# Attention and FFN in one kernel: other order of loads and clearings, gate and up weights by column halves, statistics behind the last block, twelve dummy transposes

## The reference

```python
xn = layernorm(x)                          # x: (16, 256, 256) float32, last axis 256
q, k, v = split(xn @ w_qkv)                # 16 heads of 16
attn = softmax(where(causal, q @ k.T / 4, -1e10)) @ v
a = attn @ w_out
gate, up = qdot(xn, w_gating[0]), qdot(xn, w_gating[1])   # operands cast to float8 e4m3; 256 -> 1024
f = qdot(gelu(gate) * up, w_linear)                       # 1024 -> 256
out = x + a + f
```

## Time and profile before

| | us |
|---|---|
| median of 3 runs | 421.89 (421.83 to 424.61) |
| the profiled execution, its own time | 421.3 |
| its span, first to last instruction | 419.6 |
| FFN stage up to the first matmul of `project_qk` | 103.28 |
| PE busy / DVE / ACT / POOL in the span | 371.5 / 296.7 / 223.9 / 106.9 |

### The profile page before, as it was taken

The page is one execution under the profiler, slowest core; times in us unless marked ns, Lnnn a source line. Parts: engine busy times, 40 slices in busy tenths (PEclk is TensorE's granted clock), DMA queues, the critical chain, the costliest instruction groups (busy, mean ns, idle before and its releaser), DMA issues.

```text
span 419.6 us, 9896 instructions
## 1 busy us (share of the span) xinstructions
PE 371.5 (89%) x3646; PEld 275.6 (66%) x3646; DVE 296.7 (71%) x1325; ACT 223.9 (53%) x320; POOL 106.9 (25%) x138
## 2 busy tenths in 40 slices
PE   5796589999899779999999999999999999889774
PEld 5253345556475567778788788787787787667443
DVE  5876197776545887788788888887887887787112
ACT  2773266665555145655655655556556556455540
POOL 2131033332021113322232232223323222333320
PEclk9897899999999989999999999999999999998885
DMA  7999332340717343461551642633624613300000
GB/s 244 295 352 208 110 102 100 121 181 2 247 55 252 125 160 111 139 212 47 201 180 51 229 149 80 230 113 115 228 83 148 228 49 133 104 28 2 28 25 26
DMA packets 45943, 57.58 MB, mean 137 GB/s; under 512 B 2568, under 2 KB 38984, under 8 KB 45896
## 3 DMA queue, kind: packets, MB, share of 16 engines
q1 hardware_dynamic: 45896, 56.96, 40.9%
HBM read 16.78 MB, written 12.58 MB: 70 GB/s over the span
## 4 chain that ended last, share of the span: by engine, by line
PE 68%; DVE 9%; DMA 6%; SPq 5%; issue 5%; ACT 5%; POOL 1%; POOLq 0%; ACTq 0%; DVEq 0%
PE ps L721 12%; PE ps L646 11%; PE ps L700 9%; PE ps L682 7%; PE ps L752 7%; PE ps L653 6%; PE ps L634 5%; PE ps L737 4%; DMA xt_store<-xt_part 3%; DVE act L377 3%; DMA xres<-in_L_attn_x_dram 3%; PE ps L744 2%; PE ps L614 2%; DVE masked L415 2%; SPq L192 2%
## 5 line engine op out<-in xcount | busy, mean ns | idle before, releaser
L415 DVE CUSTOM_DVE_ANT_0 masked<-ps,causal 128x256 bf16<-128x256 f32 (+1 forms) x512 | 149.1, 350 | 35.3 <-PE ps L682 35.3
L542 ACT ACTIVATE arena<-ps 128x1024 f32<-128x1024 f32 x96 | 98.7, 1028 | 76.9 <-PE ps L700 76.5
L307 POOL TENSOR_SCALAR_AFFINE_SELECT arena<-arena 128x512 f32<-128x512 f32 (+1 forms) x96 | 75.8, 789 | 191.5 <-ACT arena L542 191.5
L377 DVE TENSOR_TENSOR act<-ps,gate 128x512 fp8e4<-128x512 f32 x64 | 43.8, 684 | 18.8 <-ACT gate L495 18.0
L700 PE MATMUL ps<-stack 64*128 64x256 f32 (+1 forms) x512 | 51.7, 301 | 5.1 <-ACT arena L542 3.8
L721 PE MATMUL ps<-arena,v_aug 128*32 128x256 f32 (+1 forms) x1024 | 54.4, 343 | 1.2 <-POOL arena L307 1.2
L646 PE MATMUL ps<-xs,wq_part 128*128 128x256 f32 x384 | 53.4, 290 | 1.5 <-issue 0.7
L682 PE MATMUL ps<-stack 63*128 63x256 f32 (+1 forms) x512 | 49.1, 291 | 5.4 <-DVE row_max L415 5.4
L607 PE MATMUL ps<-x,wg 128*128 128x512 fp8e4 x128 | 40.2, 397 | 11.1 <-ACT x L483 4.9
L646 PEld LDWEIGHTS ps<-xs,wq_part 128*128 128x128 f32 x384 | 47.9, 191 | 2.7 <-ACT ffn L515 1.2
L495 ACT ACTIVATE gate<-ps 128x512 bf16<-128x512 f32 x64 | 38.1, 599 | 18.5 <-PE ps L607 14.0
(11 more groups left out here) (52 smaller groups left out, 377.1 us busy)
## 6 DMA issues: line engine op xcount, KB each, us to landing
stack<-qk_part SPq DMA_DIRECT2D x96, 256.0 KB, 2.8
xt_store<-xt_part SPq DMA_DIRECT2D x16, 512.0 KB, 4.2
xs<-xt_store SPq DMA_DIRECT2D x16, 512.0 KB, 4.1
out_dram<-w_raw SPq DMA_DIRECT2D x16, 256.0 KB, 2.8
xres<-in_L_attn_x_dram SPq DMA_DIRECT2D x1, 2560.0 KB, 13.6
arena<-in_L_ffn_w_gating_dram SPq DMA_DIRECT2D x2, 1024.0 KB, 8.6
stack<-zeros SPq DMA_DIRECT2D x4, 512.0 KB, 12.6
xres<-in_L_attn_x_dram SPq DMA_DIRECT2D x2, 512.0 KB, 12.2
```

The source lines that it names most:

```text
L307: nc.gpsimd.affine_select(diag, diag, pattern=[[0, 1024 // width], [1, P]], compare_op=ALU.is_ge, fill=0.0, base=0, channel_multiplier=-1) ...
L377: nc.vector.tensor_tensor(act8[:, j, :], up_ps[j % 2][:], gate[:, j % 2, :], ALU.mult, saturate=False).then_inc(act_done, 1)
L415: last = nc.vector.tensor_tensor_reduce(masked[:, place, i * width:(i + 1) * width], max_ps[:, place, i * width:(i + 1) * width], causal[: ...
L542: nc.scalar.activation(arena[:, n, :, :], exp_ps, ACT.Exp).then_inc(exp_done, 1)
```

## The change

On SP, the load of x for chunks 3 to 7 becomes five loads, each with its own semaphore; chunk 3's goes ahead of the store of chunk 0, chunk 4's behind `w_out`, and chunks 5 to 7 follow one in each pass over `c`. The four clearings are spread in the same way, one behind the stores of chunks 1 to 4. The gate and up weights are loaded by halves of the hidden columns, each transfer holding gate and up of 512 columns; x of chunk 1 goes between the halves. DVE casts the first half of both and the second half of up; ACT casts the second half of gate, behind gelu 1 of chunk 0. PE waits for the second half ahead of `j = 4`.

On DVE, `normalize(c + 1, .)` stands behind products 0, 2, 4 and 6, and all four `find_stats(c + 2, .)` behind product 7; `split_xt(0)` stands behind product 0 of chunk 0; the split of the attention's weights moves to the end of chunks 2 to 5. ACT does both `x8` copies before it waits for `xt_stored`. One memset of `v_aug` and that of `zeros` go from DVE to POOL. POOL's scaling of `w_raw` goes from the end of chunk 0 to the end of chunk 1. PE runs 12 dummy transposes more, behind the transposes of chunk 0.

The loads, the clearings and POOL's part (`half` in `load_wg` is a slice of 512 columns; shortened lines are marked by "..."):

```diff
-        x_in = [sem(f"x_in{i}") for i in range(3)]
+        x_in = [sem(f"x_in{i}") for i in range(CHUNKS - 1)]
...
-        wg_cast = sem("wg_cast")
+        wg_cast = [sem(f"wg_cast{i}") for i in range(2)]
...
-            for i in range(2):
-                sp.dma_start(wg_raw[:, i], w_gating[i].rearrange("(k p) n -> p k n", p=P)).then_inc(wg_in[i], 16)
+            def load_wg(i):
+                half = slice(i * HID // 2, (i + 1) * HID // 2)
+                sp.dma_start(wg_raw[:, :, :, half].rearrange("p g k n -> p (g k) n"),
+                             w_gating.rearrange("g (k p) n -> p (g k) n", p=P)[:, :, half]).then_inc(wg_in[i], 16)
+
+            load_wg(0)
             load_x(1, 1, x_in[0])
+            load_wg(1)
             sp.dma_start(wl_raw, w_linear.rearrange("(j p) n -> p j n", p=P)).then_inc(wl_in, 16)
             load_x(2, 1, x_in[1])
...
+            load_x(3, 1, x_in[2])
...
             store_xt(0)
-            load_x(3, CHUNKS - 3, x_in[2])
             sp.dma_start(w_raw[:, :, 0:3 * D], w_qkv.rearrange("(k p) n -> p k n", p=P)).then_inc(wq_in, 16)
             sp.dma_start(w_raw[:, :, 3 * D:4 * D], w_out.rearrange("(k p) n -> p k n", p=P)).then_inc(wq_in, 16)
-            sp.wait_ge(v_ones, 4)
-            for i in range(NB):
-                sp.dma_start(stack[i][3:P:4, :, :, :].rearrange("p j a s -> p (j a) s").bitcast(F32),
+            load_x(4, 1, x_in[3])
+            for c in range(1, CHUNKS - 3):
+                store_xt(c)
+                if c + 4 < CHUNKS:
+                    load_x(c + 4, 1, x_in[c + 3])
+                if c == 1:
+                    sp.wait_ge(v_ones, 4)
+                sp.dma_start(stack[c - 1][3:P:4, :, :, :].rearrange("p j a s -> p (j a) s").bitcast(F32),
                              zeros[:, :].unsqueeze(1).broadcast_to([2 * DH, 2 * PAIRS, S])).then_inc(stack_zero, 16)
-            store_xt(1)
             sp.wait_ge(stack_zero, 16 * NB)
             for i in range(NB):
                 sp.dma_start(stack[i][ROW:P:64, :, 1, :].bitcast(F32),
...
-            for c in range(2, CHUNKS - 3):
-                store_xt(c)
...
-                if at(c, 0):
+                if at(c, 1):
 
                     pool.wait_ge(wq_in, 32)
                     nc.gpsimd.tensor_scalar(w_raw[:, :, 0:D], w_raw[:, :, 0:D], Q_SCALE, None, ALU.mult).then_inc(wq_scaled, 1)
...
+            nc.gpsimd.memset(zeros[:, :], 0.0).then_inc(v_ones, 1)
+            nc.gpsimd.memset(v_aug[2][:, :, :, :], 1.0).then_inc(v_ones, 1)
             ffn_steps(step, lambda b: None)
```

DVE:

```diff
-            for i in range(3):
+            for i in range(2):
                 nc.vector.memset(v_aug[i][:, :, :, :], 1.0).then_inc(v_ones, 1)
-            nc.vector.memset(zeros[:, :], 0.0).then_inc(v_ones, 1)
             for i in range(CT):
                 find_stats(0, i)
             aggregate(0)
             for i in range(CT):
                 normalize(0, i)
-            dve.wait_ge(wg_in[1], 16)
-            nc.vector.tensor_copy(wg8[:, 1], wg_raw[:, 1], saturate=False).then_inc(wg_cast, 1)
+            dve.wait_ge(wg_in[0], 16)
+            half = slice(0, HID // 2)
+            nc.vector.tensor_copy(wg8[:, :, :, half], wg_raw[:, :, :, half], saturate=False).then_inc(wg_cast[0], 1)
             for i in range(CT):
                 find_stats(1, i)
+            dve.wait_ge(wg_in[1], 16)
+            half = slice(HID // 2, HID)
+            nc.vector.tensor_copy(wg8[:, 1, :, half], wg_raw[:, 1, :, half], saturate=False).then_inc(wg_cast[1], 1)
             aggregate(1)
-            split_xt(0)
+
...
             def step(c, has_next, has_stats):
...
-                    if has_next and j < CT:
-                        normalize(c + 1, j)
-                    if has_stats and j >= CT:
-                        find_stats(c + 2, j - CT)
-                    if 1 <= c <= 4 and j == 6:
-
-                        cols = slice((c - 1) * D, c * D)
-                        dve.wait_ge(wq_hi_done, c)
-                        for k in range(KD):
-                            last = nc.vector.tensor_tensor(by_row(wq_part[:, 1, k, cols], c - 1), by_head(w_raw[:, k, cols], c - 1),
-                                                           by_row(wq_part[:, 0, k, cols].bitcast(F32), c - 1), ALU.subtract)
-                        last.then_inc(wq_split, 1)
+                    if c == 0 and j == 0:
+                        split_xt(0)
+                    if has_next and j % 2 == 0:
+                        normalize(c + 1, j // 2)
+                if has_stats:
+                    for i in range(CT):
+                        find_stats(c + 2, i)
                 if has_next:
                     split_xt(c + 1)
                 if has_stats:
                     aggregate(c + 2)
+                if 2 <= c <= 5:
+                    split_wq(c - 2)
```

ACT and PE:

```diff
-            act.wait_ge(wg_in[0], 16)
-            nc.scalar.copy(wg8[:, 0], wg_raw[:, 0], saturate=False).then_inc(wg_cast, 1)
-
...
                     nc.scalar.copy(x8[:, k, :], xt_ps[k][:], saturate=False).then_inc(x8_done, 1)
-                    if k == 0 and not (isinstance(c, int) and c == 0):
-                        act.wait_ge(xt_stored, 16 * (C // S) * c)
+                if c >= 1:
+                    act.wait_ge(xt_stored, 16 * (C // S) * c)
+                for k in range(KD):
                     nc.scalar.copy(xt_part[:, 0, k, :], xt_ps[k][:]).then_inc(xt_hi, 1)
...
+                    if at(c, 0) and j == 1:
+                        half = slice(HID // 2, HID)
+                        act.wait_ge(wg_in[1], 16)
+                        nc.scalar.copy(wg8[:, 0, :, half], wg_raw[:, 0, :, half], saturate=False).then_inc(wg_cast[1], 1)
                     if at(c, 0) and j >= J // 2:
...
-                    if 1 <= c <= 4 and j == 4:
-
-                        if c == 1:
+                    if 2 <= c <= 5 and j == 4:
+
+                        if c == 2:
                             act.wait_ge(wq_scaled, 1)
-                        cols = slice((c - 1) * D, c * D)
+                        cols = slice((c - 2) * D, (c - 1) * D)
...
                         last.then_inc(wq_hi_done, 1)
...
-            for i in range(WARM_UP):
-                nc.tensor.transpose(gate_ps[0][:, 0:P], ident[:], ident[:])
+            def keep_warm(n):
+                for i in range(n):
+                    nc.tensor.transpose(gate_ps[1][:, 0:P], ident[:], ident[:])
+
+            keep_warm(WARM_UP)
             transpose_x(0)
-            pe.wait_ge(wg_cast, 2)
+            keep_warm(12)
+            pe.wait_ge(wg_cast[0], 1)
...
+                    if not started and j == J // 2:
+                        pe.wait_ge(wg_cast[1], 2)
```

More of the change, by code:

```diff
@@ L322, in find_stats @@
                     dve.wait_ge(x0_in[i // 2], 16)
-                elif i == 0 and isinstance(c, int):
-                    dve.wait_ge(x_in[min(c, 3) - 1], 16)
-                if i == 0 and not isinstance(c, int):
-                    dve.wait_ge(x_in[2], 16)
+                elif i == 0:
+                    dve.wait_ge(x_in[c - 1], 16)
                 ins = nc.vector.bn_stats(stats[:, i, :], tile(c, i))
@@ L364, in _, with split_wq @@
                 normalize(0, i)
-            dve.wait_ge(wg_in[1], 16)
-            nc.vector.tensor_copy(wg8[:, 1], wg_raw[:, 1], saturate=False).then_inc(wg_cast, 1)
+            dve.wait_ge(wg_in[0], 16)
+            half = slice(0, HID // 2)
+            nc.vector.tensor_copy(wg8[:, :, :, half], wg_raw[:, :, :, half], saturate=False).then_inc(wg_cast[0], 1)
             for i in range(CT):
                 find_stats(1, i)
+            dve.wait_ge(wg_in[1], 16)
+            half = slice(HID // 2, HID)
+            nc.vector.tensor_copy(wg8[:, 1, :, half], wg_raw[:, 1, :, half], saturate=False).then_inc(wg_cast[1], 1)
             aggregate(1)
-            split_xt(0)
+            def split_wq(i):
+                cols = slice(i * D, (i + 1) * D)
+                dve.wait_ge(wq_hi_done, i + 1)
+                for k in range(KD):
+                    last = nc.vector.tensor_tensor(by_row(wq_part[:, 1, k, cols], i), by_head(w_raw[:, k, cols], i),
+                                                   by_row(wq_part[:, 0, k, cols].bitcast(F32), i), ALU.subtract)
+                last.then_inc(wq_split, 1)
             def step(c, has_next, has_stats):
@@ L500, in step @@
                         nc.scalar.copy(wl8[:, rows, :], wl_raw[:, rows, :], saturate=False).then_inc(wl_cast, 1)
-                    if 1 <= c <= 4 and j == 4:
-                        if c == 1:
+                    if 2 <= c <= 5 and j == 4:
+                        if c == 2:
                             act.wait_ge(wq_scaled, 1)
-                        cols = slice((c - 1) * D, c * D)
+                        cols = slice((c - 2) * D, (c - 1) * D)
                         for k in range(KD):
-                            last = nc.scalar.copy(by_row(wq_part[:, 0, k, cols], c - 1), by_head(w_raw[:, k, cols], c - 1))
```

(16 more changed lines are left out.)

## The result

The changed kernel takes 410.39 us (median of 4 runs, 408.92 to 413.38) against 422.76 of the kernel before, measured beside it: ratio 0.9711, 95% interval 0.9637 to 0.9785. In a later set of runs, on chip 5, it took 412.50 (6 runs, 410.28 to 413.97) against 420.47: 0.9812 (0.9774 to 0.9849). The profiled execution took 413.38 us, its span 411.6, at a mean granted clock of 0.965.

A forecast was written before the change was run, and what follows sets the result against it. It took the FFN's stops for a late store and scaled weights, about 13 us in chunks 1 and 2, as the bound; savings over chunks 0 to 6 summed to 17.7 off the 421.89 median: 404.2 us, range 401.4 to 409.5.

The forecast's parts named there:

- The queue: SP's loads and stores: chunk 1's store, with no clearing ahead, lands in 4.2 us instead of 11.91.
- third rival: Stores stay slow at 11.91 us, four chunks stop 2.4 each: 413.8; chance 0.05, plus 0.04 for slower than before.
- Both waits go: Chunk 1: waits for the late store and for POOL's scaled weights vanish; chunk 1 falls from 23.56 to 11.5 us.
- the price of an undisturbed chunk: FFN chunks 1 to 5: between 11.3 and 11.8 us each, since DVE needs 0.77 us a block, under PE's 0.86.
- The adds: POOL's residual adds at a chunk's start: come later too and still meet the first normalisation; no size given.
- The tail of DVE: Chunk's end: statistics and split, 1.75 us more, fit under the down matmuls with about 1 us left.
- fourth rival: DVE's tail doesn't fit and every chunk pays 1.0 to 1.75 us at its start: 408 to 411; chance 0.06.
- Chunk 0: First FFN chunk: -0.2 us, between -1.0 and +3, with product 1 at 17.3 as before.
- first rival: Chunk 0 falls back to the low clock from 18 us on, +2.9 us: 407.1; chance 0.13.
- second rival: Chunk 0: ACT's table load costs 1.4 us more than its 1.28 ahead of `x8`: 405.6; chance 0.06.
- The attention as long as before: After the FFN: the attention stage hangs on the FFN's end as a block and keeps its length.

The follow-up runs named there:

- e6: Changed kernel with x of chunks 3 to 7 again as one load behind store 0 and all four clearings ahead of store 1; 422.12 us, 1.0019 of the kernel before.
- e7: Changed kernel with the attention weights scaled at the end of chunk 0 and rounded and split in chunks 1 to 4; 411.68 us.
- e1: Changed kernel with the next chunk's normalisations back behind products 0 to 3, statistics still behind product 7; 407.81 us.
- e5: Changed kernel with POOL's residual adds cut to one column, leaving most output without the FFN's part; 408.03 us.
- e2: Changed kernel with the next chunk's normalisations behind products 2 to 5; 403.64 us, 0.9608 of the kernel before.
- the repeated one: Second profile of the unedited changed kernel, taken beside the kernels with filler dummies; that profiled run took 412.27 us.

## Why the prediction was wrong

The direction and the cause of the gain were right. The size was not: 410.39 against 404.2, above the range's 409.5. (The range's lower end is 401.6 by its own terms, not 401.4.)

- **The queue** held. Chunk 1 no longer stops, and neither does chunk 2; e6, which puts the old order back, undoes all of the gain. The third rival (stores slow) is refuted: 4.6 us, and no wait.
- **"Both waits go"** held. That the move of the scaling has a part in it did not (e7); the sum gave it no term of its own.
- **The failed step is the price of an undisturbed chunk, put between 11.3 and 11.8 us; chunks 1 to 4 took 13.14, 13.57, 12.79 and 12.36.** It averaged DVE's work over a chunk ((0.92 + 0.61) / 2 = 0.77 us a block, under PE's 0.86) and concluded that DVE was off the path. Its mean was under PE's, but the last normalisation had moved from product 3 to product 6, and only one product comes between it and the transposes, which wait for all four. That was never set beside PE's time for the transposes, though the order of the instructions showed it. Price: 3.7 us in seven chunks, gone in e1.
- **The adds.** I named the 0.81 us of the first normalisation as a cost before, wrote that the adds "come later too and still meet it", and put no term for it in the sum. They met it for up to 1.40 us, and the block it holds is the one whose up matmuls need product 1. Price: 2.9 in chunks 1 to 5, by the lengths of the normalisations and by e5; gone in e2.
- **The rest is 0.9 us**: e2, with neither delay, ends its FFN at 104.92, where the forecast's sum gives 121.71 - 17.7 = 104.0. It is 0.4 in chunk 1 and 0.6 in chunk 2, less 0.7 in chunk 0, and 0.0 to 0.3 in each other; in chunk 3 the rounding and split of the k weights have a part, put at 0.2 (it takes 0.45 more than chunk 4). With 0.7 for the normalisations of chunk 0 (15.82 to 14.33 in e2, less 0.8 of its gap), 3.7 + 2.9 + 0.7 + 0.9 = 8.2 are found of the 8.4 us that the FFN stage was short (112.41 - 104.0).
- **The tail of DVE** (fourth rival): wrong as a mechanism. e2 keeps the tail and runs chunk 4 at 11.64. The rival's time (408 to 411) met the measured one by another cause.
- **Chunk 0** had 26.76 as its end and got 27.49. Product 1 at 17.38 was foreseen (17.3). The normalisation ahead of it took 1.10 us, beside POOL's memsets, and the transposes waited for the last one; with the normalisations behind products 2 to 5 it ends at 26.06 (e2).
- **The low clock in chunk 0** (first rival, +2.9 us at 0.13) occurs in three of twelve profiles; in the repeated one it cost 1.25 us, with 1.08 of late weights beside it. It was wrong to treat it as either or. How much it widens the runs (408.92 to 413.97) isn't shown: the slowest of the first set, 413.38, is the profiled one, and its chunk 0 reads 1.00.
- **The table load** ran at 9.16 for 1.28 us, and the `x8` copy followed at 10.45. The Trainium skill (ScalarE: Activation LUTs, What ACT_TABLE_LOAD costs) adds about 1380 ns of drain; this trace shows none, so the second rival is refuted.
- **"The attention as long as before"**: 299.2 against 297.9 in the profiles. Between executions it varies with the clock by more than that.

## What to carry to other kernels

Look for the last small step on a side engine that the next stage waits for as a whole, and count the time from it, not the engine's mean per block: the same four instructions cost 7.5 us by their place alone (112.41 to 104.92). An in-order queue pays for the order of its entries, so put what is needed soonest ahead; here that was the whole gain, 2.9% in one set of runs and 1.9% in the other. Keep short VectorE steps that have a product behind them away from the time in which GpSimd reads and writes tensors.
